# One image's entropy model moved beside the next image's projection, with its input read back from DRAM

## The reference, cut to what matters

```python
def _gn(v, G=32, eps=1e-5):          # mean and variance over 6 channels and all pixels of an image
    ...
# layer 0: self-attention over the 4096 pixels of an image; q, k have 24 channels, v has 192
q = prelu(conv1x1(x, w1, b1), a1); k = prelu(conv1x1(x, w2, b2), a2); v = prelu(conv1x1(x, wa, ba), aa)
score = softmax(einsum('bnc,bcm->bnm', q, k), axis=2)
out = einsum('bnm,bmc->bnc', score, v)
# layer 1: per channel a small network 1 -> 3 -> 3 -> 3 -> 1 on x - 0.5 and on x + 0.5
for i in range(4):
    logits = einsum('cij,cjn->cin', softplus(ms[i]), logits) + bs[i]
    if i < 3: logits = logits + tanh(fs[i]) * tanh(logits)
sign = -sign(lower + upper)
likelihood = maximum(abs(sigmoid(sign * upper) - sigmoid(sign * lower)), 1e-6)
# the whole
x = x + layer0(_gn(x))
x = x + layer1(_gn(x))
```

## Time and profile before

| | |
|---|---|
| timed runs | 5570.25 us median of 3 (5567.03 to 5574.96) |
| profiled execution, span of core 0 | 5558.5 us |
| timed median minus that span | 11.8 us |
| mean granted TensorE clock | 0.959 |
| busy: PE, DVE, ACT, POOL | 5034.0, 4522.2, 3898.3, 689.0 us |
| moved by DMA | 200.42 MB |

### The profile page before, as it was taken

The page is one execution under the profiler, slowest core; times in us unless marked ns, Lnnn a source line. Parts: engine busy times, 40 slices in busy tenths (PEclk is TensorE's granted clock), DMA queues, the critical chain, the costliest instruction groups (busy, mean ns, idle before and its releaser), DMA issues.

```text
span 5558.5 us, 97185 instructions
## 1 busy us (share of the span) xinstructions
PE 5034.0 (91%) x35200; PEld 3298.7 (59%) x35200; DVE 4522.2 (81%) x5627; ACT 3898.3 (70%) x4404; POOL 689.0 (12%) x630
## 2 busy tenths in 40 slices
PE   6998989989899898998989989899898998889988
PEld 4885258852588525885258842688426884268842
DVE  6886888868888688886878868888687886888877
ACT  4667866678666786667866678666786667866677
POOL 5000220002200022000220012200122001210012
PEclk9999999999899998999999999899998999999999
DMA  1002410024100241002400024000240002400033
GB/s 42 2 2 42 97 37 2 2 48 97 32 2 2 48 104 24 2 2 52 102 22 2 2 59 97 20 2 2 59 97 20 2 2 59 97 20 2 2 70 67
DMA packets 64910, 200.42 MB, mean 36 GB/s; under 512 B 17201, under 2 KB 17842, under 8 KB 50610
## 3 DMA queue, kind: packets, MB, share of 16 engines
q1 hardware_dynamic: 64434, 193.73, 16.0%
HBM read 25.70 MB, written 25.17 MB: 9 GB/s over the span
## 4 chain that ended last, share of the span: by engine, by line
PE 51%; issue 33%; POOL 8%; DVE 5%; ACT 1%; DMA 1%; SPq 0%; POOLq 0%; DVEq 0%; ACTq 0%
PE ps L1040 11%; PE ps L1038 11%; PE ps L1042 11%; PE ps L998 7%; PE ps L945 7%; POOL arena L440 2%; POOL arena L434 2%; PE ps L1090 2%; POOL arena L424 2%; DVE mxp L705 1%; PE ps L1098 1%; DVE arena L773 1%; PE ps L990 1%; DMA arena<-xn 1%; ACT arena L558 0%
## 5 line engine op out<-in xcount | busy, mean ns | idle before, releaser
L1040 PE MATMUL ps<-arena 128*128 128x192 f16 x8192 | 2039.3, 249 | 0.0
L1038 PE MATMUL ps<-arena 128*128 128x193 f16 x8192 | 2031.0, 248 | 4.8 <-DVE arena L773 4.8
L1042 PE MATMUL ps<-arena 128*128 128x193 f16 x8192 | 2022.5, 247 | 0.0
L508 ACT ACTIVATE arena<-ps 128x1024 f16<-128x1024 f32 x1024 | 1048.9, 1024 | 952.2 <-PE ps L998 952.1
L773 DVE TENSOR_TENSOR arena<-arena 128x1024 f16<-128x1024 f32 x1024 | 1247.2, 1218 | 253.2 <-ACT arena L512 253.2
L705 DVE TENSOR_REDUCE mxp<-ps 128x1 f32<-128x512 f32 x1792 | 1193.0, 688 | 132.3 <-PE ps L945 120.0
L833 DVE SCALAR_TENSOR_TENSOR arena<-arena,w_all,ps 96x1024 f32<-96x1024 f32 x768 | 952.6, 1272 | 283.2 <-ACT arena L565 273.2
L512 ACT ACTIVATE arena<-ps 128x1024 f32<-128x1024 f32 x1024 | 1044.7, 1020 | 0.0
L565 ACT ACTIVATE arena<-ps,w_all 96x1024 f32<-96x1024 f32 x768 | 833.9, 1103 | 192.2 <-PE ps L1098 128.9
L1040 PEld LDWEIGHTS ps<-arena 128*128 128x128 f16 x8192 | 800.8, 98 | 268.8 <-issue 6.6
L1090 PE MATMUL ps<-arena,w_all 128*96 128x512 f32 x1536 | 757.0, 617 | 149.4 <-ACT arena L558 99.0
(11 more groups left out here) (113 smaller groups left out, 3636.1 us busy)
## 6 DMA issues: line engine op xcount, KB each, us to landing
arena<-xn SPq DMA_DIRECT2D x384, 256.0 KB, 4.4
x_sb<-x_dram SPq DMA_DIRECT2D x16, 1536.0 KB, 9.8
arena<-x_sb SPq DMA_DIRECT2D x384, 64.0 KB, 4.1
out_dram<-arena SPq DMA_DIRECT2D x96, 256.0 KB
arena<-arena SPq DMA_DIRECT2D x96, 128.0 KB, 2.4
arena<-arena SPq DMA_DIRECT2D x64, 64.0 KB, 2.1
arena<-mrows SPq DMA_DIRECT2D x64, 3.0 KB
wv_sb<-wv_dram SPq DMA_DIRECT2D x1, 144.0 KB
```

What stands on the lines that cost most here:

```text
L508: act.activation(e_hi[:, q % 4, :].rearrange("p (k n) -> p k n", k=2), sc, ACT.Exp)
L1038: pe.matmul(acc, eh, v_sb[:, m, 0:C + 1], start=(m == 0 and t % 2 == 0), stop=False, skip_group_check=True)
L1040: pe.matmul(acc[:, 0:C], eh, v_sb[:, m, VW:VW + C], start=False, stop=False, skip_group_check=True)
L1042: ins = pe.matmul(acc, el, v_sb[:, m, 0:C + 1], start=False, stop=(m == MT - 1), skip_group_check=True)
```

## The change

The program is written anew in two phases. `phase_a(l, proj)` is the entropy model of image l together with the projection of image l + 1; `phase_b(b, l)` is the attention of image b. The sequence is projection of image 0, attention of image 0, then seven times (phase_a, phase_b), then the entropy model of the last image alone.

- The norms no longer write `xn`. The first is folded into the projection's weights (`w_s`) and a bias row, the second into scale and biases of the first tanh and into a factor on the first matmul's weights (`gn2`, seven more DVE steps and 6 small matmuls).
- The entropy model's input goes through DRAM: each attention block's sum is stored to `x2d` (`store_x2`), and phase A loads it with a broadcast into 4 copies (`load_x4`), once more into rows of `t0` after the tanh (`load_side`), and a third time for the final sum (`load_res`).
- A unit is 16 channels by 4096 pixels; there are 12 units and 48 slots as before, and tanh and gate work on 128 x 1024 instead of 96 x 1024. `side` is gone from DVE.
- The two middle layers are matmuls of 64 rows by 64 columns: four for each layer and slot instead of two, one in each quarter of the array.
- Of the projection ACT computes one part (`negative`), DVE the PReLU from PSUM (`value`), and POOL all fp16 splits (`queries`, three operations of 128 x 512; `values`, two of 128 x 384). It has 2 PSUM banks instead of 4. POOL also takes the difference of the sigmoids.
- In the slots of phase A, slots 0 to 13 each carry one bank of v, slots 18 to 33 each a pair of maximum tiles. DVE takes the statistics of the next image in the attention (2 of 96 x 512 for each block), and the whole first norm runs in the last block.
- POOL's coefficients at the start are for 12 units: 125 dependent steps and 96 products for the weights.

```diff
-            def image(b, row, last):
...
-                    for k in range(4):
-                        sp.dma_start(x4[k * G:(k + 1) * G, s, :], xn[c0:c0 + G, half, s * UN:(s + 1) * UN]
-                                     ).then_inc(x4_in[s], 16)
-                    if u >= 3:
-                        store(b, row, u - 3)
+            def load_x4(l, row, v):
+                u, half = v // 2, v % 2
+                src = x2d[bass.ds(row + u * UC, UC), :].rearrange("c (a n) -> a c n", a=2)
+                for a in range(2):
+                    sp.dma_start(x4[64 * a:64 * a + 64, v % 2, :],
+                                 src[a, :, half * HC:(half + 1) * HC].unsqueeze(0).to_broadcast([4, UC, HC])
+                                 ).then_inc(x4_in[v % 2], 16)
+            def load_side(l, row, v):
+                u, half = v // 2, v % 2
+                sp.wait_ge(t0_ready, l * SLOTS + 2 * v + 2)
+                for a in range(2):
+                    col = a * (HW // 2) + half * HC
+                    sp.dma_start(t0[64 * a + 48:64 * a + 64, v % T0R, :, :],
+                                 x2d[bass.ds(row + u * UC, UC), col:col + HC].unsqueeze(1).to_broadcast([UC, 2, HC])
+                                 ).then_inc(side_in[v % T0R], 16)
+            def chunked(dram, row, u):
+                return dram[bass.ds(row + u * UC, UC), :].rearrange("c (a k n) -> k a c n", a=2, n=N)
+            def load_res(l, row, u):
+                if u >= XR:
+                    sp.wait_ge(stored[u % XR], l * (UNITS // XR) * 64 + u // XR * 64)
+                src = chunked(x2d, row, u)
+                for k in range(CHUNKS):
+                    sp.dma_start(res[k * 32:(k + 1) * 32, u % XR, :], src[k]).then_inc(res_in[u % XR], 16)
+            def store(l, row, u):
+                sp.wait_ge(res_ready, l * UNITS + u + 1)
+                dst = chunked(out_rows, row, u)
+                for k in range(CHUNKS):
+                    sp.dma_start(dst[k], res[k * 32:(k + 1) * 32, u % XR, :]).then_inc(stored[u % XR], 16)
...
+                    for v in range(HALVES):
+                        load_side(l, row, v)
+                        if v + 2 < HALVES:
+                            load_x4(l, row, v + 2)
+                        if v >= 8 and v % 2 == 0:
+                            store(l, row, v // 2 - 4)
+                        if v % 2 == 1:
+                            load_res(l, row, v // 2)
...
+                def queries(n):
+                    pool.tensor_copy(parts, p_val[:, n % 2, :]).then_inc(qk_hi, 1)
...
+                    pool.tensor_scalar(parts, parts, cols_sb[:, COL_M:COL_M + 1], None, ALU.mult).then_inc(qk_hi, 1)
...
+                    pool.tensor_tensor(parts, parts, p_val[:, n % 2, :], ALU.add).then_inc(qk_done, 1)
...
+                def value(n):
+                    w, col = (N, COL_A) if n < QK else (2 * C, COL_AA)
+                    dve.wait_ge(neg_ready, pj(BANKS, n + 1))
+                    if n >= 2:
+                        if n - 2 < QK:
+                            dve.wait_ge(qk_done, pj(QK, n - 1))
+                        else:
+                            dve.wait_ge(v_done, pj(VB, n - 1 - QK))
...
-                        for d in range(2):
-                            ins = pe.matmul(ps[0:HR, 2 * (s % 3) + d, :], w_all[:, u // 2, 0:HR],
-                                            t0[:, u % 2, d, k * N:(k + 1) * N], start=True, stop=True)
+                    for k in range(2):
+                        for a in range(2):
+                            ins = pe.matmul(ps[64 * k:64 * k + 64, at + a, :], w1s[64 * a:64 * a + 64, u, :],
+                                            t0[64 * a:64 * a + 64, v % T0R, d, k * N:(k + 1) * N],
+                                            start=True, stop=True)
```

More of the change, by code:

```diff
@@ L73, with tile_uses, tile, program @@
 SETUP_STEPS = 9 + 2
[L74 to L80, removed]
-MAX_STEPS = 6
[L82 to L102, removed]
+GN1_STEPS = 13
+GN2_STEPS = 18
+MAX_STEPS = 6
+def tile_uses():
+    uses = []
+    for s in range(SLOTS + 2):
+        if s < SLOTS:
+            uses.append(("h1", s))
+        if 1 <= s <= SLOTS:
+            uses.append(("h2", s - 1))
+        if s >= 5 and (s - 1) % 4 == 0:
+            uses.append(("h3", (s - 1) // 4 - 1))
+    return uses
+USES = tile_uses()
+SPOT = {use: n for n, use in enumerate(USES)}
+def tile(kind, i):
+    return FIRST_TILE + 2 * (SPOT[kind, i] % 3)
+def program(nc, x, wall, cols, g6, sel, eye, diag, mraw, fraw, braw, x2d, out):
     x_rows = x.rearrange("b c h w -> (b c) (h w)")
@@ L337, in store @@
[L337 to L347 removed]
+                sp.dma_start(xp[0:HALF, h, :], x_rows[h * HALF:(h + 1) * HALF, :]).then_inc(x_in[h], 16)
@@ new lines, in _ @@
+            phase_a(None, None, True)
+            phase_b(0, 0, C, None)
+            with sp.Fori(0, B - 1) as l:
+                row = sp.compute_val(l * C)
+                phase_a(l, row, True)
+                phase_b(sp.compute_val(l + 1), sp.compute_val(l * C + C), sp.compute_val((l + 2) % B * C), l)
+            phase_a(B - 1, (B - 1) * C, False)
+            for u in range(UNITS - 3, UNITS):
+                store(B - 1, (B - 1) * C, u)
+            for s in range(XR):
+                sp.wait_ge(stored[s], B * (UNITS // XR) * 16 * CHUNKS)
@@ L892, in image @@
-                result(UNITS - 2)
-                if not last:
-                    for j in range(6, BLOCKS):
-                        statistics(following, 1, j)
-                    first_norm(following)
-                result(UNITS - 1)
-            for j in range(BLOCKS):
-                statistics(0, 1, j)
-            first_norm(0)
-            with dve.Fori(0, B - 1) as b:
-                image(b, False)
-            image(B - 1, True)
+            dve.wait_ge(x_stat, 1)
+            for _ in gn1(0):
+                pass
@@ L922, in image, with averages @@
-            def image(b, last):
-                def bank_free(n):
-                    if n >= 4:
-                        pe.wait_ge(proj_act, b * BANKS + n - 3)
-                for n in range(QK_BANKS):
+            def averages(step_sem, base, k, mm, means, spread, bank):
+                pe.wait_ge(step_sem, base + (1 if k == 0 else 5))
+                pe.matmul(ps[0:HALF, bank + k, 0:2], g6_sb[:, :], means if k == 0 else spread, start=True, stop=True
+                          ).then_inc(mm, 1)
@@ L1115, in image @@
-                if not last:
-                    averages(pe.compute_val(b + 1), 0)
-            averages(0, 0)
-            with pe.Fori(0, B - 1) as b:
-                image(b, False)
-            image(B - 1, True)
+            for k in range(2):
+                averages1(0, k)
+            shifts(0)
+            phase_a(None, True)
+            phase_b(0, None)
+            with pe.Fori(0, B - 1) as l:
+                phase_a(l, True)
+                phase_b(pe.compute_val(l + 1), l)
+            phase_a(B - 1, False)
```

1393 lines of the change are left out of this document (782 added, 611 removed).

## The result

The changed kernel takes 5910.21 us (median of 4, 5904.53 to 5910.98), against 5572.60 us (5567.03 to 5575.21) for the kernel before: ratio 1.0611, 95% interval 1.0596 to 1.0626, 338 us slower. The profiled execution has a span of 5902.6 us.

The account below looks back on a forecast made before the run. It took entropy-stretch transfers sharing the first DMA engine as the bound: 190 + 383 + 7 x (312 + 385) + (237 + 74) = 5763 us span, 5775 with 12 added; own range 5460 to 6550, 8 in 10 5180 to 6350.

Parts of the forecast that it names:

- part 1: PE in the entropy slots: four 64x64 matmuls overlap across row quarters, 0.86 us a layer, 4.05 us a slot.
- part 2: Projection beside the slots: 3.2 us a q/k bank, first gate 33 us after attention, attention again after 238 on compute alone.
- part 3: Attention: the added statistics are hidden in pairs 14 and 15; it takes 385 us.
- part 4: Start and end: POOL's coefficients precede the queries, first attention at 190 us; last entropy model without projection 237 us.
- part 5: Entropy-stretch transfers: few-engine transfers share the lowest engines; first engine carries 256 us, attention again after 312 us (273 to 408).
- Rival A: Few-engine transfers spread over different engines, or engines exceed 25 GB/s; load spread gives 5183 us; chance 0.25 together with C.
- Rival B: Middle layers in the slots: row quarters do not overlap, 3.44 us a layer, 6407 us in all; chance 0.08.
- Rival C: POOL's q/k chain takes what the slots win: 4.1 us a bank, 8 us an image, 5250 us; chance 0.25 with A.
- the sum: Whole kernel on compute alone: 190 + 383 + 7 x (238 + 385) + 237 = 5171 us, 5183 with 12 added.

Follow-up runs that it names:

- few transfers: Changed kernel with most entropy-stretch x4, side and residual loads and stores, and their waits, left out; all computing kept: 5319.16 us.
- combination 2: Changed kernel with residual transfers and x4 copies each in eight, coefficient setup behind first projection, q/k split ended by VectorE, first side load before second stack group: 5298.58 us.
- x4 in 8: Changed kernel with each half's x4 load as eight plain copies of 16 rows instead of two broadcast transfers: 5468.91 us.
- residual in 8: Changed kernel with each unit's residual loads and stores as eight transfers of 16 rows instead of four of 32: 5433.54 us.
- q/k on VectorE: Changed kernel with the query/key bank split done by GpSimd's cast and one VectorE operation instead of three GpSimd operations: 5871.21 us.

## Why the prediction was right

| step | predicted | measured |
|---|---|---|
| a layer of four 64x64 matmuls (part 1) | 0.86 us | 1.09 at full clock |
| slots on compute alone, 48 (parts 1, 2) | 201 us | 48 x 4.18 = 201 (few transfers) |
| q/k bank on GpSimd (part 2) | 3.2 us | 3.6 |
| first gate of DVE after attention (part 2) | 33 us | 44.9 first, 48.6 mean |
| attention again after it, compute alone | 238 us | 253.2 (few transfers) |
| attention (part 3) | 385 us | 387.8 (389.5 in few transfers) |
| first attention starts (part 4) | 190 us | 203.2 |
| after the last attention, compute alone | 237 us | 231.8 (few transfers) |
| whole, compute alone | 5183 us | 5319.16 (few transfers) |
| first side load after attention (part 5) | 26 us | 35.6 first, 39.1 mean |
| first engine, first side load to last x4 landing (part 5) | 256 us | 622.4 to 878.4: 256.0 |
| attention again after it | 312 us | 323.4 first, 326.3 mean |
| after the last attention | 311 us | 316.6 |
| what the transfers add | 5775 - 5183 = 592 us | 5910 - 5319 = 591 |
| whole | 5775 us | 5910.21 |

The deciding step, part 5, holds in kind and size: transfers of few engines share the lowest ones, and their load sets when attention starts again. The completions of the x4 loads show the sharing; two edits that spread the transfers, and one that leaves most of them out, show what it costs. Rival A (few-engine transfers on different engines) is what the cut kernels look like, and not the changed one. Rival B is out: row quarters run side by side, 1.09 us a layer for the 3.44 without. Rival C's chain exists (3.6 us a bank for 3.2, 3 us in eight banks) and is worth the few us that it said.

That the 256 us came out to the decimal is luck, for its terms are off both ways. An engine reads DRAM at 25 GB/s here too, 2.6 us for 64 KB and not 3.0: the loads were priced some 24 us too high. The side loads, at 28 us for 44 (0.64 us each, a price for which the prediction gives no working), were priced too low: by the estimate of 1.0 us above they take 44. The stores were right. With the measured prices the terms make 248 us, and the remaining 8 are close to the 7 us in which the trace shows only one packet under way. The transfers set the pace from the first unit on: the first four take 79 us here and 68.7 with few transfers.

The 135 us that the forecast was short lie elsewhere, and most of them in the start of the stretch. In span it was short by 140: 14 until the end of the first attention, 7 x 14.3 between attentions, 7 x 2.8 in attention, 6 after the last one. (The time lies 8 us above the span, not 12.) Of the 14.3, 13 are one term: the first side load is issued 39.1 us after attention ends (35.6 the first time) and not 26. The same delay is in the compute terms, where the first gate comes at 48.6 us and not 33: the kernel with few transfers shows it, and behind the first gate it keeps the sum (253.2 - 48.6 = 204.6 us, 205 predicted). GpSimd's product of 128 x 512 in f16 takes 1.57 us and its cast 0.61, together more than the 1.9 assumed for the pair; in six of the seven images its first cast comes 6.1 to 7.7 us after the end of attention and not 3.2 as in the first; and the first side load, which the sum didn't place in SyncE's order, stands behind the second stack group, which waits for the eighth bank. The first image:

```profile
617.33 1.17 POOL L471 TENSOR_TENSOR kq<-kq,p_val 128x512 f16<-128x512 f16 x1
618.52 0.50 SPq L324 DMA_DIRECT2D kst<-kq  x1
622.39 0.91 SPq L296 DMA_DIRECT2D arena<-x2d  x2
628.55 1.99 PE L1073 MATMUL ps<-arena,w1s 64*64 64x512 f32 x8 [14.06 <-DMA arena<-x2d]
631.75 1.28 DVE L856 SCALAR_TENSOR_TENSOR th<-th,gates,ps 128x1024 f32<-128x1024 f32 x1 [12.60 <-ACT th L592]
```

Mending the bank and the order takes 7 of these 16 us off (combination 2). The start misses by 13 us in another place:

```profile
39.31 0.22 POOL L407 TENSOR_TENSOR th<-th 128x12 f32<-128x12 f32 x1 [33.27 <-DVE eye L710]
106.24 0.71 POOL L465 CAST kq<-p_val 128x512 f16<-128x512 f32 x1
165.98 1.03 PE L1161 MATMUL ps<-kst,qst 128*128 128x512 f16 x2 [1.39 <-DVE mxp L899]
167.12 1.23 DVE L899 TENSOR_REDUCE mxp<-ps 128x2 f32<-128x1024 f32 x1 [1.20 <-PE ps L1161]
```

GpSimd's setup takes the 67 us of the sum, but it begins at 39.3 and not at 26.3, since it waits for VectorE's part of the setup: the last of its constants have landed 9.6 us later than in the kernel before (28.67, for 19.05), and its operations are on 456 columns and not 228. Behind it two terms cancel. The banks of v come 1.4 us apart and not 1.9, 7 us less in all. The maximum pairs come 2.4 us apart and not 1.9, 7 us more, as the matmuls of a pair (1.03 us) and its reduction (1.23) take turns; the granted clock is 0.54 from 158 to 195, and the sum had 0.6 us for a pair, which is what two such matmuls take at full clock (0.61 us at 908.7).

What the transfers add hits within 1 us by luck as well, though the step behind it is good. Between attentions they add 326.3 - 253.2 = 73.1 us for the 74 of the forecast. At the end they add 85 for 74, each attention is 1.7 us shorter with them than without (the cause is open), and the spans differ by 584 us, the medians by 591.

## What to carry to other kernels

Count for every transfer how many DMA engines its shape lets it use, and add up the bytes that fall on the lowest of them for one steady unit of the loop: a DMA share of 0.27 can be a full engine. If it is full, cut the transfers along a dimension that spreads them, and then watch the issuer, for each cut moves work to its queue: here 36 issues a unit filled SyncE, and giving the stores to an idle engine won another 1.2%. As long as such a resource sets the end, ask of an earlier start whether the whole row of its transfers moves with it: it was kept where it did (4.2 us gave 4.4), and worth nothing where only the first transfer moved (7.2 us gave none). And when two sums agree to the microsecond, check their terms one by one.

## What was not expected of the hardware

An issue isn't free of what it issues to. In the steady units of the changed kernel SyncE's issues of 64 KB stores take 0.70 to 2.8 us, and four of them 7.2 us together. The same four stores to the same two engines take 0.61 to 0.70 us each and 2.9 together in "x4 in 8", where the x4 loads are off these engines; eight of 32 KB, cut and spread ("residual in 8"), take 0.37 each in the median and 3.6 to 3.9 together. That they wait for room in the queues of full engines is the likely reading, and wasn't tested by itself. The longest, 7.15 us, stands right behind the loads of the next image, and there "x4 in 8" has one of 6.4 us too.

GpSimd's cast of 128 x 512 to f16 takes 0.61 us in the changed kernel, and 1.00 us when VectorE's new operation on `kq` runs beside it (q/k on VectorE; beside other VectorE operations it still takes 0.61 there), which goes some way to explain the 2.9 us a bank.

A side load is dear to the engines that are full: 8 KB on each of 16 engines, 0.33 us at 25 GB/s, and by the estimate above 1.0 us on the first. Why the packets slow down beside it was not tested.
